# A decoder layer on one core: VectorE clears one value buffer, and SyncE issues its bulk transfers at another place of each step

## What is computed

```python
def self_attention(x):                     # 16 heads of 8 columns
    qkv = (x * ln_g + ln_b) @ w_qkv + b_qkv
    scores = q @ k.T * 8 ** -0.5 + rel_bias[i - j]
    return softmax(scores) @ v @ w_out + b_out
def cross_attention(x, ctx, mask):
    scores = (x @ Wq.T + bq) @ (ctx @ Wk.T + bk).T * 8 ** -0.5
    scores = where(mask == 0, -1e9, scores)
    return softmax(scores) @ (ctx @ Wv.T + bv) @ Wo.T + bo
def ffn(x):                                # 128 -> 512 -> 128
    return bitlinear(silu(bitlinear(x, w_gate)) * bitlinear(x, w_up), w_down)
x = x + self_attention(layernorm(x))
x = x + cross_attention(layernorm(x), ctx, mask)
x = x + ffn(layernorm(x))
```

## Time and profile before

| | |
|---|---|
| median of 3 runs | 456.83 us (456.45 to 457.15) |
| profiled execution | 452.96 us, its span 451.1 us |
| busy, share of the span | PE 86%, DVE 85%, ACT 77%, POOL 68% |
| DMA | 67.19 MB, mean 149 GB/s |
| longest SyncE waits | for the store's result 37.8 us, for the parts of X 35.2 and 34.1 us |

### The profile page before, as it was taken

One profiled execution on the slowest core, in us unless ns is written; L12 is line 12 of the kernel. 1 busy time (PEld: TensorE's weight loads), 2 busy tenths in 40 slices (PEclk: granted clock), 3 DMA queues, 4 the chain that ended last, 5 costly groups with the idle time before them and its releaser, 6 DMA issues. The chain is left out here.

```text
span 451.1 us, 16947 instructions
## 1 busy us (share of the span) xinstructions
PE 385.8 (86%) x5436; PEld 312.2 (69%) x5468; DVE 381.2 (85%) x1922; ACT 346.4 (77%) x962; POOL 308.2 (68%) x783
## 2 busy tenths in 40 slices
PE   3348878999999999999989999999999999866662
PEld 2236667778887888788878887888778877544541
DVE  4954757789999999999989998999999999787643
ACT  2125676889998999999988998999889988775441
POOL 6554586878777778778876777778778766565120
PEclk9998998999999999999999999999999999998885
DMA  6576476666667566756676657576766553323000
GB/s 195 147 186 170 107 218 169 178 157 175 175 160 199 150 180 157 197 155 177 156 183 138 184 155 186 156 179 150 193 160 167 166 146 90 87 78 102 8 6 12
DMA packets 100171, 67.19 MB, mean 149 GB/s; under 512 B 73269, under 2 KB 90421, under 8 KB 100085
## 3 DMA queue, kind: packets, MB, share of 16 engines
q1 hardware_dynamic: 98209, 64.08, 54.6%
q10 hardware_dynamic: 1876, 2.03, 1.4%
HBM read 46.08 MB, written 19.07 MB: 144 GB/s over the span
## 5 line engine op out<-in xcount | busy, mean ns | idle before, releaser
L976 DVE CUSTOM_DVE_ANT_0 biased<-bank,mask_bias 128x128 bf16<-128x128 f32 x512 | 114.9, 285 | 13.0 <-PE bank L1245 12.8
L981 DVE TENSOR_REDUCE neg_max_S<-bank 128x4 f32<-128x512 f32 x128 | 87.4, 684 | 16.3 <-PE bank L1245 15.5
L664 ACT ACTIVATE probs_X<-bank 128x512 f32<-128x512 f32 x128 | 71.6, 586 | 13.4 <-PE bank L1263 12.8
L664 ACT ACTIVATE probs_S<-bank 128x512 f32<-128x512 f32 x128 | 75.1, 593 | 8.4 <-PE bank L1263 7.8
L1245 PE MATMUL bank<-stack_k_S,stack_q_S 120*128 120x128 bf16 x512 | 52.0, 226 | 6.1 <-DMA stack_k_S<-scratch_S 5.0
L1245 PE MATMUL bank<-stack_k_X,stack_q_X 72*128 72x128 bf16 x512 | 49.9, 221 | 7.3 <-DMA stack_k_X<-scratch_X 6.1
L1263 PEld LDWEIGHTS bank<-stack_q_X,stack_k_X 74*128 74x128 bf16 x512 | 40.5, 99 | 16.3 <-issue 1.6
L1263 PE MATMUL bank<-stack_q_X,stack_k_X 74*128 74x128 bf16 x512 | 50.7, 222 | 0.0
L1260 PE MATMUL bank<-ident_bf,mask_bias 128*128 128x512 bf16 x128 | 50.1, 392 | 0.0
L1263 PE MATMUL bank<-stack_q_S,stack_k_S 122*128 122x128 bf16 x512 | 47.4, 224 | 2.5 <-DMA stack_q_S<-neg_maxT_S 1.9
L1245 PEld LDWEIGHTS bank<-stack_k_S,stack_q_S 120*128 120x128 bf16 x512 | 40.7, 104 | 8.5 <-issue 5.8
(11 more groups left out here) (165 smaller groups left out, 1120.9 us busy)
## 6 DMA issues: line engine op xcount, KB each, us to landing
stack_q_S<-scratch_S SPq DMA_DIRECT2D x32, 288.0 KB
stack_k_S<-scratch_S SPq DMA_DIRECT2D x32, 288.0 KB
stack_q_X<-scratch_X SPq DMA_DIRECT2D x32, 288.0 KB
stack_k_X<-scratch_X SPq DMA_DIRECT2D x32, 288.0 KB
scratch_S<-qk_parts_S SPq DMA_DIRECT2D x32, 192.0 KB, 3.0
scratch_X<-qk_parts_X SPq DMA_DIRECT2D x32, 192.0 KB, 2.5
ctxT<-ctx SPq DMA_DIRECT2D x8, 256.0 KB, 3.0
scratch_S<-qk_parts_S SPq DMA_DIRECT2D x32, 64.0 KB, 2.6
```

Source lines behind the costliest of these rows:

```text
L664: act.activation(probs[a][:, b % 2, c, :], bank_b[c % 2][:, :], ACT.Exp).then_inc(sems["exp_" + a], 1)
L976: last = dve.tensor_tensor_reduce(biased[:, c, hh, :], quarter(bank_a[c % 2], hh), mask_bias[:, b % 2, :], -1.0, -2.0 * BIG, ALU.add, ALU.min,
L981: dve.tensor_reduce(neg_max[a][:, first_head(c):first_head(c) + 2 * HC - 1:2], bank_a[c % 2][:, :].rearrange("i (h j) -> i h j", h=HC), AX ...
```

## The change

VectorE clears self attention's value buffer, as the first thing it does, where GpSimd cleared it before; the semaphore `v_cleared` tells ScalarE, and the counts of GpSimd's constants shrink by two. On SyncE the bulk transfers move: in `fill` behind `stack_in` of S, in `ramp` and `step` behind `stack_in` and `max_in` of X and ahead of `stack_in` of S.

```diff
@@ constants @@
-ONES, IDENT, V_AUG_S, POOL_CONST = 2, 5, 13, 16
+ONES, IDENT, MAX_ROWS_S, POOL_CONST = 2, 5, 11, 14
...
@@ SyncE @@
             def fill(st):
                 max_in("S", st, 1)
-                load_c(st, -2)
                 parts_again("S", st, -1)
                 parts_out("S", st, -1)
-                load_x(st, -1)
                 if st.at(-1):
                     rel_rows(sp, stack_q)
                 if st.at(0):
                     rel_copies(sp)
                 stack_in("S", st, -1)
+                load_c(st, -2)
+                load_x(st, -1)
 
             def ramp(st):
                 max_in("S", st, 1)
                 parts_out("X", st, 1)
-                load_x(st, -1)
-                store(st, 14)
                 parts_again("S", st, -1)
-                load_c(st, 0)
                 parts_out("S", st, -1)
                 stack_in("X", st, 1)
                 max_in("X", st, 2)
+                load_x(st, -1)
+                store(st, 14)
+                load_c(st, 0)
                 stack_in("S", st, -1)
                 parts_again("X", st, 0)
 
             def step(st):
-                store(st, 5)
                 parts_out("X", st, 1)
                 max_in("S", st, 1)
-                load_x(st, -1)
-                load_c(st, -1)
                 parts_again("S", st, -1)
                 parts_out("S", st, -1)
                 stack_in("X", st, 1)
                 max_in("X", st, 2)
+                store(st, 5)
+                load_x(st, -1)
+                load_c(st, -1)
                 stack_in("S", st, -1)
                 parts_again("X", st, 0)
@@ GpSimd @@
             def clear_values(a):
-                const(pool.memset(v_aug[a][:], 0.0))
-                const(pool.memset(v_aug[a][:, :, :, 0:4:3, HD:HD + 1], 1.0))
+                if a == "X":
+                    const(pool.memset(v_aug[a][:], 0.0))
+                    const(pool.memset(v_aug[a][:, :, :, 0:4:3, HD:HD + 1], 1.0))
                 const(pool.memset(neg_max_parts[a][:], 0.0))
...
@@ ScalarE, v_out, batch 0 @@
-                        act.wait_ge(sems["pool_const"], V_AUG_S if a == "S" else POOL_CONST)
+                        if a == "S":
+                            act.wait_ge(sems["v_cleared"], 2)
+                        else:
+                            act.wait_ge(sems["pool_const"], POOL_CONST)
@@ VectorE, ahead of everything else @@
+            dve.memset(v_aug["S"][:], 0.0).then_inc(sems["v_cleared"], 1)
+            dve.wait_ge(sems["v_cleared"], 1)
+            dve.memset(v_aug["S"][:, :, :, 0:4:3, HD:HD + 1], 1.0).then_inc(sems["v_cleared"], 1)
@@ TensorE, max_transposed, batch 0 @@
-                        pe.wait_ge(sems["pool_const"], V_AUG_S)
+                        pe.wait_ge(sems["pool_const"], MAX_ROWS_S)
```

More of the change, by code:

```diff
@@ L187, in layer @@
             "amax_y y_step y_inv y_q yT_ps yT gate_half h_unit gate_up tanh h_gate h amax_h "
-            "h_step h_inv h_scale down_scale h_q hT_ps hT down out_stored ffn_sums"
+            "h_step h_inv h_scale down_scale h_q hT_ps hT down out_stored ffn_sums v_cleared"
         ).split()
@@ L352, in ramp @@
                 parts_out("X", st, 1)
-                load_x(st, -1)
-                store(st, 14)
-                parts_again("S", st, -1)
-                load_c(st, 0)
[L357 to L363, removed]
-                store(st, 5)
-                parts_out("X", st, 1)
-                max_in("S", st, 1)
-                load_x(st, -1)
-                load_c(st, -1)
                 parts_again("S", st, -1)
@@ L372, in step @@
                 max_in("X", st, 2)
+                load_x(st, -1)
+                store(st, 14)
+                load_c(st, 0)
+                stack_in("S", st, -1)
+                parts_again("X", st, 0)
+            def step(st):
+                parts_out("X", st, 1)
+                max_in("S", st, 1)
+                parts_again("S", st, -1)
+                parts_out("S", st, -1)
+                stack_in("X", st, 1)
+                max_in("X", st, 2)
+                store(st, 5)
+                load_x(st, -1)
+                load_c(st, -1)
                 stack_in("S", st, -1)
@@ L638, in _ @@
             clear_values("S")
-            assert n == V_AUG_S
+            assert n == MAX_ROWS_S
             run(begun, fill, ramp, step, drain)
```

## The result

The changed kernel took 460.79 us (median of 22 runs, 457.17 to 470.25) against 456.03 us for the kernel before on the same chip: a ratio of 1.0125, with a 95% interval of 1.0104 to 1.0147. It is slower by 1.25%, some 5.7 us; the forecast was 460.4 us. The ratios leave out the slow executions of either kernel, so 1.0125 is not the ratio of the two medians, 1.0104. The profiled execution took 459.81 us at a span of 458.0 and a mean clock of 0.957 (452.96, 451.1 and 0.967 before).

The account below looks back on a forecast made before the run. Bound: a start where each step waits for the one before, then steps filled by TensorE and VectorE. 1.2 + 0.8 + 4.25 + 0.6 - 3.2 = +3.65 us; 456.83 + 3.6 gives 460.4 us, range 455 to 465.5.

Parts of the forecast that it names:

- the 6.85 us of the sum: Start of the kernel: forecast loss from the x loads behind the stacks, 1.2 + 0.8 + 4.25 + 0.6 us.
- The clear: Start: VectorE's clear, about 2 us, costs nothing before x lands; batch 0's parts are issued 1.3 to 2.1 us earlier.
- First and second load: Steps -1 to 0: x loads behind the stacks hold groups 3 and 4; batch 1's maxima +1.2 us, range -0.8 to +2.4.
- the third load: Step 1: x load between batch 2's stack and batch 1's maxima costs 0 to 1.2 us, taken as 0.8.
- Fourth load: Step 2: x load behind batch 3's stack holds VectorE's group 6, then TensorE and all behind; +4.25 us, landing 4.3.
- The half clock: Start: longer idle time may bring back the granted clock of 0.50 seen at 43 to 44 us; left in the range.
- Sixth load: Step 4: x load behind the stack of X delays group 8 and X's maxima; 0 to 2.3 us, taken as +0.6.
- Steady steps: Steady part: TensorE's waits for the stack of X behind bulk transfers mostly go; a gain of 3.2 us taken.
- The sign named for it: Steady part: the forecast is right if TensorE's X stack waits, 6.1 us before, shrink to about 3 us.
- The stack of S, feared 0.4 us late: Steady steps: two bulk transfers ahead make S at worst 0.4 us late in each of seven steps, a 2.8 us loss.
- the faster one: First rival, chance 0.18: loads land in 3.3 us even behind a stack, mainly step 2; 454.6 us.
- The late stack of S: Third rival, chance 0.10: S stack late in the steady part, +2.8 in place of -3.2; 466.5 us.

## Why the prediction was right, and where its terms were off

The direction and the mechanism held: x loads behind the stack arrive too late in the first steps, the steady steps win, and the first outweighs the second. The difference was forecast as +3.6 us and came out as +5.7 by the ratio. It is that close because two errors cancel in part: the start cost more than the 6.85 us of the sum (10.5 us, 8 to 13, between the changed kernel and the one with the steady steps alone), and the steady steps gave more than 3.2. That the time itself came within 0.4 us of the forecast is luck besides: the kernel before measured 456.03 in these runs, not the 456.83 that the forecast was built on.

- *The clear.* Right. VectorE's clear took 1.76 us, ended before x came, and cost nothing. One CAST ran free in 0.29 us, between the two ends given, and the parts were issued 2.00 us earlier, inside 1.3 to 2.1. The stack's second half moved by 2.64 (20.32 to 17.68), where 2.0 was taken and 2.5 was the far end.
- *First and second load, +1.2.* The waits came where they were forecast, and the first load landed after 5.2 us, taken as 5.3; the price was lower: batch 0's row maxima start 0.23 us earlier than before (26.90 against 27.13), batch 1's 0.30 later (35.81 against 35.51), both inside the range given. With the third load, +0.8, the sum was +2.0 at batch 1's second scores; +0.70 was measured there. By the ratios, 2.6 us of the 11.8 of all x loads are left after the fourth and the sixth, with a range of some 4 us either way, so no price of these loads is shown.
- *Fourth load, +4.25: the mis-sized term.* Its own wait was sized well. At full clock, batch 1's transposes follow its second scores by 6.37 us with the load ahead of the stack (50.31 - 43.94) and by 10.91 with it behind (55.13 - 44.22): 4.54 us. The landing, taken as 4.3, was 4.3 to 4.8 in the three other kernels that issue it by SyncE behind the stack. In the changed kernel's profile it was 6.0, and the stack's own issue was later by another 1.4 us (from second scores to the load 5.74 us against 4.32), because these scores ran at half clock and the stack's buffer came free late. Putting this one load back gave 7.1 us.
- *The half clock.* Named in the prediction and "left in the range", not in the sum. Filling the wait gave 3.8 us by the runs and 2.4 us by the timeline. This is about what the 4.25 lacks of the 7.1: this stall of 7.58 us on TensorE cost more than its own length.
- *Sixth load, +0.6.* Measured 2.1 us (0.2 to 4.0, the kernel with this load put back), inside the 0 to 2.3 given. VectorE did not take the wait back: it waited 4.10 us with all of the ramp behind it.
- *Steady steps, -3.2.* Right in place; -4.8 by the runs of these steps alone (interval -7.0 to -2.6, which holds 3.2), and -7.4 (4 to 11) between the kernel with the clear alone and the one with clear and steady steps. The sign named for it, X stack waits of about 3 us, came, but the clear alone brought them to 3.9; the gain is shown by the ratio, not by the waits. The stack of S, feared 0.4 us late, kept its margin: in a step with store and context ahead of it, it is issued 7.51 us before its first scores (rows below), against 8.6 before, and nothing waits. What I counted as two bulk transfers a step is at most that; x is all loaded by then.

```profile
242.65 0.41 SPq L335 DMA_DIRECT2D out<-x_all  x1
243.11 0.51 SPq L321 DMA_DIRECT2D ctxT<-ctx  x1
...
244.57 0.76 SPq L299 DMA_DIRECT2D stack_k_S<-scratch_S  x1
...
252.08 0.39 PE L1253 MATMUL bank<-stack_k_S,stack_q_S 120*128 120x128 bf16 x4
```
(Timeline of the changed kernel, SyncE and TensorE.)

Of the rivals, the faster one needed landings under 3.8 us: 3.2 us was seen only with the load ahead of the stack (the kernel with the fourth load put back). The late stack of S did not come. The sum of the three parts run alone, -0.18 + 3.12 - 1.06 = +1.88%, is above the +1.25% of all together; the intervals of the parts are wide enough for that, and the 3.12 may hold the stretch at half clock near the end. I leave open whether the parts help each other.

## What to carry to other kernels

Before a prefetch is moved behind another instruction of an in-order issuer, ask what that instruction waits for: here the load had no wait of its own and inherited that of a stack whose buffer was still in use, with the DMA engines idle. The same edit can be a gain in the steady part and a loss in the start, so cost it, and keep it, stage by stage. A long wait on TensorE has two prices, its length and the lower clock behind it; put empty matmuls into it to see how much of the second there is (3.8 us behind the wait of 7.58 here, nothing that shows behind 1.6 and 1.0). And one pair of profiles is a poor scale for a few microseconds: identical first steps came out 3 us apart.

## What the runs showed of the hardware

- VectorE clears 128x2048 fp32 in 1.76 us, about what GpSimd takes (1.80). The cast of 128x256 to bf16 took 0.29 us with no GpSimd clear under way and 1.39 beside one.
- The same 256 KB load, behind the same stack, landed after 4.3, 4.6, 4.8 and 6.0 us in four kernels; one landing is a poor price for a sum.
- Where TensorE waited 5.45 to 7.58 us ahead of batch 1's transposes (four kernels), the granted clock behind the wait was 0.50; with the wait filled it was 1.00.
- The half clock at 43 to 47 us is not the change's alone: before has it, behind a wait of 0.92 us for the maxima, though none of the five other kernels with the old place of the x loads does. With the new place it came where that wait was longest (1.75, 1.85, 1.91 and 3.07 us) and stayed away where it was 0.38 to 1.31, so that one wait does not decide it.
